# A graph layer on one core: five buffers for gathered rows, three for product rows and three for matrix rows

## The reference

```
xn = layernorm(x)
msgs = xn[src]
u = xn @ root + bias
for r in range(8):                       # 8 relations
    mask = (edge_type == r)
    sums = segment_sum(msgs * mask, dst) # over the edges into a node
    u += (sums / max(cnt_r, 1)) @ weight[r]
z = concat([u, xn]) @ w_gate + b_gate
h = tanh(u) * z + xn * (1 - z)
x = x + h + linear_attention(xn)
x = x + ffn_fp4(layernorm(x))
```

## Time and profile before

| | |
|---|---|
| median of 3 runs | 1604.83 us (1604.75 to 1608.31) |
| the profiled execution: device time | 1601.57 us |
| its span, first to last instruction | 1599.8 us |
| mean granted clock of PE | 0.994 |
| busy share: PE, DVE, ACT, POOL | 97%, 55%, 26%, 50% |

### The profile page before, as it was taken

How to read it: one execution, slowest core, us unless ns; L and a number is a source line. 1 busy time by engine, 2 the same in 40 slices (tenths; PEclk the granted TensorE clock), 3 DMA queues, 4 the chain that set the end, 5 groups by cost and what they waited for, 6 DMA issues and landing times.

```text
span 1599.8 us, 19058 instructions
## 1 busy us (share of the span) xinstructions
PE 1545.8 (97%) x7138; PEld 1252.4 (78%) x7138; DVE 885.9 (55%) x1329; ACT 412.4 (26%) x597; POOL 806.3 (50%) x700
## 2 busy tenths in 40 slices
PE   7999999999999999999999999999999999998998
PEld 6987777777778678888888888888877778878886
DVE  5353223444442220004888877885577766779886
ACT  5411112222222112113222222322311123243321
POOL 5327776667563136557545545555555543333220
PEclk9999999999999999999999999999999999999999
DMA  6332233333323123228767777777989894450001
GB/s 223 109 102 75 77 95 90 109 97 108 91 87 115 66 80 100 83 78 289 261 223 262 242 250 259 271 263 229 323 316 310 297 321 171 173 169 16 40 40 50
DMA packets 120459, 262.48 MB, mean 164 GB/s; under 512 B 23451, under 2 KB 37010, under 8 KB 120360
## 3 DMA queue, kind: packets, MB, share of 16 engines
q1 hardware_dynamic: 48568, 109.34, 20.2%
q0 software_dynamic: 33056, 83.02, 17.3%
q10 hardware_dynamic: 38736, 68.83, 11.6%
HBM read 193.33 MB, written 80.06 MB: 171 GB/s over the span
## 4 chain that ended last, share of the span: by engine, by line
PE 70%; DVE 16%; DMA 5%; issue 4%; POOL 2%; ACT 2%; ACTq 0%; SPq 0%; DVEq 0%; POOLq 0%
PE ps L1863 56%; PE ps L2104 4%; DMA source_rows<-relation_rows,row_list 3%; PE ps L2113 2%; DMA u_sum<-u_rows 2%; DVE u_sum L1604 2%; PE ps L1990 2%; PE ps L1946 1%; PE ps L1970 1%; PE ps L1982 1%; DVE source_rows_lo L1588 1%; ACT source_rows_hi L2340 1%; DVE wq_rows L589 1%; POOL xf L1037 1%; DVE xf L1753 1%
## 5 line engine op out<-in xcount | busy, mean ns | idle before, releaser
L1863 PE MATMUL ps<-WH,XTH 128*128 128x512 f32 (+1 forms) x1680 | 666.3, 397 | 0.5 <-DVE XTL L1099 0.5
L1863 PE MATMUL ps<-WH,XTL 128*128 128x512 f32 (+1 forms) x1680 | 651.9, 388 | 0.0
L1863 PE MATMUL ps<-WL,XTH 128*128 128x512 f32 (+1 forms) x1680 | 651.9, 388 | 0.0
L878 POOL TENSOR_TENSOR WL<-RAW,WH 128x512 fp32r<-128x512 f32 x176 | 234.5, 1334 | 271.3 <-ACT WH L2252 269.2
L1863 PEld LDWEIGHTS ps<-WH,XTH 128*128 128x128 f32 x1680 | 318.2, 189 | 66.8 <-issue 7.1
L1863 PEld LDWEIGHTS ps<-WH,XTL 128*128 128x128 f32 x1680 | 316.3, 188 | 64.5
L1863 PEld LDWEIGHTS ps<-WL,XTH 128*128 128x128 f32 x1680 | 317.1, 189 | 60.6 <-issue 2.4
L934 POOL DMA_INDIRECT source_rows<-relation_rows,row_list x180 | 217.9, 1211 | 244.0 <-DVE u_sum L1604 127.6
L2280 ACT ACTIVATE EV<-ps 128x512 f32<-128x512 f32 x180 | 107.5, 597 | 626.3 <-PE ps L1863 565.5
L955 POOL DMA_INDIRECT edge_lists<-edge_words x160 | 196.8, 1230 | 46.4 <-issue 44.4
L1604 DVE SCALAR_TENSOR_TENSOR u_sum<-source_rows,weight_list,u_sum 128x1024 f32<-128x1024 f32 x120 | 163.0, 1358 | 49.2 <-DMA source_rows<-relation_rows,row_list 39.1
(11 more groups left out here) (316 smaller groups left out, 1518.5 us busy)
## 6 DMA issues: line engine op xcount, KB each, us to landing
relation_rows<-EV ACTq DMA_DIRECT2D x160, 256.0 KB, 2.2
RAW<-in_L_gnn_weight SPq DMA_DIRECT2D x128, 256.0 KB, 2.9
u_rows<-u_sum SPq DMA_DIRECT2D x20, 512.0 KB, 5.5
RAW<-in_L_gnn_w_gate SPq DMA_DIRECT2D x32, 256.0 KB, 4.8
mix_rows<-mix_rows_out ACTq DMA_DIRECT2D x10, 512.0 KB, 2.6
root_rows<-EV ACTq DMA_DIRECT2D x20, 256.0 KB, 5.0
u_sum<-u_rows SPq DMA_DIRECT2D x10, 512.0 KB, 6.8
bias_rows<-root_rows SPq DMA_DIRECT2D x10, 512.0 KB, 6.1
```

Of the source, the lines that this page charges most:

```text
L878: g.tensor_tensor(WL[:, h % 2, k, 0:w], RAW[:, q % 4, 0:w], WH[:, h % 2, k, 0:w].bitcast(F32), ALU.subtract).then_inc(w_lo, 1)
L1863: mm = t_.matmul(ps[:, bank, 0:w], a[:, t, k, :], b[:, s, k, 0:w], start=(k == 0 and j == 0), stop=(k == KT - 1 and j == 2))
```

## The change

The ring of gathered rows gets a fifth buffer (RING 4 to 5). The memory for it comes from two other rings and from padding: the ring of product rows has three buffers in place of four (`EVS`), and the ring of matrix rows three in place of four (`RAWS`). All indices, semaphores and counts follow. Two further things come with the new places in memory. The `NAT` buffers now begin 2 KB inside the low part of the gate matrix, so the pieces of the feed-forward weights use the buffers in another rotation, and the fourth piece waits until PE has transposed the first. The first blocks of the queries' matrix are spread over both of its areas differently.

```
-RING = 4
+RING = 5
+EVS = 3
+RAWS = 3
...
-        EV = keep("EV", [P, 2, D], F32)
-        XG, = stage_tensors(("source_rows", [P, 4, D], F32R))
+        EV, = stage_tensors(("EV", [P, 2, D], F32))
+        EVR = keep("product_rows", [P, EVS, HW], F32)
+        XG, = stage_tensors(("source_rows", [P, RING, D], F32R))
...
+        below_th = keep("below_th", [P, HW], F32)
         TH = keep("TH", [P, 2, KT, P], F32R)
         TL = keep("TL", [P, 2, KT, P], F32R)
+        below_w = keep("below_w", [P, HW], F32)
...
-        RAW = keep("RAW", [P, 4, HW], F32)
-        RAW4, = stage_tensors(("w_rows_first", [P, 4, HW], F32))
+        RAW = keep("RAW", [P, RAWS, HW], F32)
+        RAW4, = stage_tensors(("w_rows_first", [P, KT - RAWS, 3 * HID], F32))
...
         def ev_slot(s):
-            return EV[:, s // 2, HW * (s % 2):HW * (s % 2) + HW]
+            return EVR[:, s, :]
         def ev_stores(n):
-            return 16 * (n // 4 + 1)
+            return 16 * (n // EVS + 1)
...
             def load_raw(q):
                 h, k = q // KT, q % KT
                 if q >= KT:
-                    sp.wait_ge(w_lo, q - 3)
+                    sp.wait_ge(w_lo, RAWS if q < KT + RAWS else q - RAWS + 1)
...
-                while raw_next < KT * min(h + 1, NH) + min(t, KT) + 4 and raw_next < KT * (NH + 1) + 4:
+                while raw_next < KT * min(h + 1, NH) + min(t, KT) + RAWS and raw_next < KT * (NH + 1) + RAWS:
                     load_raw(raw_next)
                     raw_next += 1
...
-            for n in range(4):
+            for n in range(3):
                 load_nat(n)
-            for n in range(4, len(NAT_TILES)):
-                sp.wait_ge(wt_ps, n - 3)
+            for n in range(3, len(NAT_TILES)):
+                sp.wait_ge(wt_ps, max(n - 3, 1))
                 load_nat(n)
...
-                need(act, ev_out[s], 16 * (n // 4))
+                need(act, ev_out[s], 16 * (n // EVS))
```

More of the change, by code:

```diff
@@ L323, in gps_layer @@
         xtl_ready = sem("xtl_ready")
-        raw_in = [sem(f"raw_in{s}") for s in range(4)]
+        raw_in = [sem(f"raw_in{s}") for s in range(RAWS + 1)]
         raw_first = sem("raw_first")
@@ L330, in gps_layer @@
         ev = sem("ev")
-        ev_out = [sem(f"ev_out{s}") for s in range(4)]
+        ev_out = [sem(f"ev_out{s}") for s in range(EVS)]
         dve_e = sem("dve_e")
@@ L476, in raw_count @@
         def raw_count(q):
-            return 16 * (2 + max(q // 4 - 1, 0))
+            return 32 if q < KT else 16 * (2 + (q - KT) // RAWS + 1)
         def raw(q):
-            return RAW[:, q % 4, 0:w_cols(q // KT)] if q < 4 or q >= KT else RAW4[:, q % 4, 0:w_cols(0)]
+            return RAW4[:, q - RAWS, :] if RAWS <= q < KT else RAW[:, q % RAWS, 0:w_cols(q // KT)]
         def prod_bank(n):
@@ L643, in load_raw @@
                 if q >= KT:
-                    sp.wait_ge(w_lo, q - 3)
+                    sp.wait_ge(w_lo, RAWS if q < KT + RAWS else q - RAWS + 1)
                 if h == 0:
-                    landed = raw_in[q] if q < 4 else raw_first
+                    landed = raw_in[q] if q <= RAWS else raw_first
                     sp.dma_start(raw(q)[:, 0:HID], w_q[k * P:(k + 1) * P, :]).then_inc(landed, 16)
@@ L649, in load_raw @@
                 else:
-                    sp.dma_start(RAW[:, q % 4, :], raw_rows(h, k)).then_inc(raw_in[q % 4], 16)
+                    sp.dma_start(RAW[:, q % RAWS, :], raw_rows(h, k)).then_inc(raw_in[q % RAWS], 16)
             load_x(0)
@@ L686, in load_qkv @@
                     for n in range(NT):
-                        sp.wait_ge(ev_out[n % 4], ev_stores(n))
+                        sp.wait_ge(ev_out[n % EVS], ev_stores(n))
                 elif i < NT:
@@ L727, in load_gate_rows @@
                     m = NT * (H_GATE + b) + t
-                    sp.wait_ge(ev_out[m % 4], ev_stores(m))
+                    sp.wait_ge(ev_out[m % EVS], ev_stores(m))
                 sp.dma_start(ZD[:, t % 2, :], z_d[rows(t), :]).then_inc(tile_in[t % 2], 16)
@@ L942, in gather @@
                     last = NT * (H_REL + 2 * GROUPS[m.group][1])
-                    for n in range(last - 4, last):
-                        pool.wait_ge(ev_out[n % 4], ev_stores(n))
+                    for n in range(last - EVS, last):
+                        pool.wait_ge(ev_out[n % EVS], ev_stores(n))
                 if m.index >= RING:
@@ L1010, in _ @@
             n_rounds = more_rounds(pool, round_pool, first_pool)
-            for s in range(4):
+            for s in range(RING):
                 pool.wait_ge(xg_in[s], 16 * (NCH // RING) * n_rounds + 16 * LATER)
@@ L1639, in evacuate_gate @@
             def evacuate_gate(n):
-                h, t, s = n // NT, n % NT, n % 4
+                h, t, s = n // NT, n % NT, n % EVS
                 b = h - H_GATE
@@ L1644, in evacuate_gate @@
                 dve.wait_ge(ev, n)
-                dve.wait_ge(ev_out[s], 16 * (n // 4))
+                dve.wait_ge(ev_out[s], 16 * (n // EVS))
                 v.tensor_tensor(ev_slot(s), ps[:, prod_bank(n), :], ZBIAS[:, HW * b:HW * b + HW],
@@ L2242, in hi_row @@
                 w = w_cols(h)
-                if 4 <= q < KT:
+                if RAWS < q < KT:
                     act.wait_ge(raw_first, 16 * 2 * 4)
                 else:
-                    act.wait_ge(raw_in[q % 4], raw_count(q))
+                    act.wait_ge(raw_in[q % RAWS if q >= KT else q], raw_count(q))
                 need(act, prod, NT * (h - 1))
@@ L2436, in tile_terms @@
                     act.wait_ge(wq_out, 48 * R)
-                    for n in range(NSTEP - 4, NSTEP):
-                        act.wait_ge(ev_out[n % 4], ev_stores(n))
+                    for n in range(NSTEP - EVS, NSTEP):
+                        act.wait_ge(ev_out[n % EVS], ev_stores(n))
                 need(act, x2_ready, t - 1)
```

12 lines of the change are left out of this document (6 added, 6 removed).

## The result

The changed kernel takes 1601.81 us (median of 20 runs, 1596.12 to 1607.22), the kernel before 1605.15 us in the same comparison (20 runs, 1602.78 to 1612.42). The ratio is 0.9974, with a 95% interval of 0.9965 to 0.9984: 4.2 us faster, between 2.6 and 5.6 us.

A forecast was written before the change was run, and what follows sets the result against it. PE, busy 97% of the span, was taken as the bound, with 15.6 us to win. Terms -4.4 + 1.8 + 1.1 = -1.5 us from the 1604.83 us median gave 1603.3 us, own range 1600.5 to 1606.

The forecast's parts named there:

- The fifth buffer, first regime: Up to 1173 the chain runs through gathers; earlier gathers remove PE's idle near 1176 and its slow clock: -4.4 us.
- the sign that it had named as wrong: If no gather stands in the chain but PE still stalls near 1172, something other than the ring held it.
- The fifth buffer, second regime: From 1193 on no gather is in the loop, so rounds stay at 20.7 us; only the earlier start carries through.
- What could be won: Seven tiles, 1155.03 to 1298.07: 15.6 us at most, 10.4 of PE idling and the rest a lower clock.
- The loop through the sum: From 1193: left-over's low part, POOL's low part, SP's block load, next tile's sum load; 20.7 us a round against 18.20.
- Three product buffers: Product stores land in 2.2 us and a buffer is wanted again 16 us later: no effect.
- Three matrix buffers: Last half of the gate matrix: blocks 179 and 183 load late and PE waits for POOL: +1.8 us, bounds 0 to 3.6.
- Late matrix blocks: Rival, chance 0.1: at the change of stage, chained loads of 7.5 us each make the kernel slower, 1610.3 us.
- The fourth weight piece: Feed-forward weights: issued at 1432.77 with the fifth, so PE starts it later: +1.1 us, bounds 0.8 and 2.5.
- Full DMA engines: Rival, chance 0.15: gathers issued earlier land no earlier, leaving only the costs of +2.9 us: 1607.7 us.
- Ahead and staying ahead: Rival, chance 0.2: DVE builds some 8 us of lead in the sums' stretch; bound 9.8 us less costs, 1597.9 us.
- The dissolved loop: Extreme of the faster rival, chance 0.03: the loop through the sum vanishes too, 15.6 - 2.9 = 12.7 us, 1592.1 us.

The follow-up runs named there:

- the repaired one: Kernel after, with blocks 179 and 180 put in two spare rows and the fourth weight piece loaded once the first gate half is used: 1597.81 us, ratio 0.9962.
- the unstalled kernels: Kernel after with the sum loaded one step earlier (1593.18 us), or ahead of the block load (1592.75), or earlier with both costs repaired (1589.78).
- the step moved: Kernel after with SP loading the next tile's sum at item 4 instead of 5: 1593.18 us; also with both costs repaired: 1589.78 us.
- the edit on SP: Kernel after with the next tile's sum load placed ahead of the matrix block's load in SP's queue, same step: 1592.75 us, ratio 0.9921.

## Why the prediction came out right, and which terms were off

- **The time.** 1603.3 us forecast, 1601.81 us measured, inside the forecast's own range. But both terms of the sum were too small: gain 4.4, measured 8.3; costs 2.9, measured 4.2. The errors of 3.9 and 1.3 us partly cancel. The difference to before was forecast as 1.5 us and measured as 4.2 (2.6 to 5.6), nearly three times as much. That the time still lies in the range is in part luck.
- **The fifth buffer, first regime.** "PE's idle of 2.79 us and the slow 1.56 us behind it": the slow clock went; the idle shrank to 1.97 us, since the load of the sum of 1161.86 took 8.85 us. The forecast let the gather's left-over come forward alone and did not ask what else that round's left-over stands behind. This is also the sign that it had named as wrong, no gather in the chain and PE still stalled near 1172; the gather that landed at 1171.64, where 1169.6 was forecast, says that the ring was not out of it. Over all traces the size came right: the first two of the seven tiles took 40.3 to 45.8 us with four buffers (mean 42.7, five traces) and 39.3 and 36.9 with five, 4.6 us less where 4.4 was said. Between the two profiled executions alone it is 1.6.
- **The fifth buffer, second regime.** This is the step that was mis-sized: "nothing in the loop waits for a gather ... so 20.7 us a round stays". By PE's left-over sums, five rounds took 20.0 us each with five buffers (19.97 in after, 19.88 in the repaired one) and 20.4 to 20.9 with four. Some 0.7 us a round, 3.6 us in all, for which the forecast had nothing. The traces show where it lies. Over these rounds the load of the sum took 7.1 to 7.7 us in the mean of a trace with four buffers and 6.9 and 6.8 with five, some 0.5 us a round. And once in the stretch POOL pauses for 1.84 us, where its issue takes 0.70 otherwise, with nothing that the profile shows as its reason. The chain of before and, in the second fence, that of after at the same place:

```profile
1255.21 1.30 DVE source_rows_lo L1588
1256.53 0.03 POOLq L934
1256.56 1.84 issue
```

```profile
1254.94 0.70 issue
```

In all seven traces with four buffers the pause stands at the gather behind this left-over's low part, in the loop. Where the chain runs through it, the piece from the low part to the issue of the sum's load takes 7.0 us (before: 1256.51 to 1263.47), where after takes 5.9 in all five rounds. In all five traces with five buffers the pause stands two gathers earlier (1249.64 in after), outside the loop. So about 1.1 us of the 3.6, an estimate, hang on where this pause falls in POOL's list, and not on a wait of the ring. Why the loads of the sum landed sooner isn't shown. The gather loop of 20.0 us was there too, but in the five traces with four buffers and the late load it came last only once in these rounds (a gather of 1263.08 with three product buffers). The bound of 9.8 us for the whole term did hold the 8.3; the interval goes up to 11.

- **What could be won.** 15.6 us was read from one execution whose stretch took 143.04 us. The five traces with four buffers and the late load have a mean of 145.9, so 18.5 us lay there. Of the 10.4 us of waits only 9.6 belong to it: one wait, 0.75 us at 906.66, lies in group 0, where the prediction says that there is none.
- **The loop through the sum.** Right, and shown: cutting SP's order frees all of it once the gathers have room. That PE's waits would come "all from about 1212 on" was not so: it already waits at 1174.93 and 1193.94.
- **Three product buffers.** Nothing, as said (0.9999).
- **Three matrix buffers.** The place and the chain were right (block 179, then 183, PE behind POOL). +1.8 was forecast; the ratio gives 3.4 (1.3 to 5.6), the traces by stage 2.7. The term used 4.9 us for the load of block 179, which took 5.61 us in after's chain and 6.71 in the run of this edit. That is the direction of the rival *Late matrix blocks*, short of its 7.2 us.
- **The fourth weight piece.** +1.1 forecast, 1.87 in after's trace, 2.4 (1.0 to 4.0) by the ratio and 2.4 by the traces. The first idle piece came as forecast (1.24 us), though the load that it was read from was not alone: the earlier trace rows show two issued within 1.19 us. The forecast stopped there; a second piece of 1.06 us follows. The 2.4 lies within its bound of 2.5.
- **Rivals.** *Full DMA engines* is refuted by what the fifth buffer won (8.3 us) and by 377 GB/s at a share of 1.00 with PE unstalled. The prediction's estimate of 3 us from the 358 GB/s of the Trainium skill ("DMA: Bandwidth & Descriptors", Specifications) comes to 2.5 us by its own numbers (35 us at 332 GB/s), and the 377 GB/s show that this limit did not bind. *Ahead and staying ahead* did not come, by the chain: the loop through the sum held DVE from 1161.86 on. By size alone it would not be ruled out, since its 9.8 us lie within the 6 to 11 of the fifth buffer. The dissolved loop, 12.7 us in all, came only with the edit on SP (0.9921 is 12.7 us).

How much the two separate costs add up to is not settled closely: alone they sum to 5.8 us by the ratios and 5.1 by the traces, together they measured 4.2, within their intervals. Why PE's first transposition of `u_tile` at the change of stage starts 2.9 to 3.4 us behind step 209 in the unstalled kernels (0.95 us in after, 1.4 before) is open.

## What to carry to other kernels

When a chain of waits alternates between two loops of nearly the same length, removing one uncovers the other: price a change by the next loop, and test both cuts together before dropping either. A change that adds an instruction can also move a pause of an engine on or off a loop, which is no effect of the buffer. Look at what stands behind a waiting instruction in a DMA-issuing queue: here a load that needed nothing was held by a block load ahead of it, and moving two lines won 8.5 us on top of the change's 4.2. With four buffers, the same load set one step earlier won 2.9. Read the size of a stalled stretch from more than one execution; this one varied by 7 us.

## What was not expected of the hardware

- The DMA engines showed a share of 0.91 while waits paced them, and 1.00 with 377 and 386 GB/s over 1155 to 1190 in the unstalled kernels with the step moved (368 at 0.99 with the queue's order changed). 0.91 over a window was not full.
- A stretch in which PE never waited repeated to 0.01 us (127.40 us three times), while stalled ones spread from 142.4 to 149.6 us with the same work.
- POOL paused once for 1.84 us with no wait in the profile, at the same place of its list in every kernel with four buffers and two gathers earlier in every kernel with five.
